# Decoder layer, one core: the end of a group's front moves into the network slots of the group before it

## What is computed

```python
x = layernorm(x + attn(x))                 # linear attention, 16 heads of 16, chunks of 64
x = layernorm(x + xattn(x, k, bias, ctx))  # a causal convolution over the channels
x = layernorm(x + ffn(x))                  # gate and up (256 -> 2048), gelu, product, down (2048 -> 256)

# xattn, for head size H = 16 groups of num_heads = 8 channels, all along L = 256
kv = v[:, :, :, None, :] * ctx[:, :, None, :, :]      # 8 x 8 products per group
y = causal_conv(kv, k) + kv * bias                    # the second term is the skip
out = einsum('bhijl,bhil->bhjl', y, ctx)
```

## Time and profile before

| | us |
|---|---|
| median of three runs | 573.89 (573.31 to 574.43) |
| the profiled execution | 574.71 |
| span of its instructions | 572.4 |
| PE busy in the span | 539.1 (94%) |
| DVE busy | 375.3 (66%) |
| ACT busy | 148.0 (26%) |
| POOL busy | 123.3 (22%) |

### The profile page before, as it was taken

The page is one execution under the profiler, slowest core; times in us unless marked ns, Lnnn a source line. Parts: engine busy times, 40 slices in busy tenths (PEclk is TensorE's granted clock), DMA queues, the critical chain, the costliest instruction groups (busy, mean ns, idle before and its releaser), DMA issues.

```text
span 572.4 us, 9307 instructions
## 1 busy us (share of the span) xinstructions
PE 539.1 (94%) x3385; PEld 439.7 (77%) x3385; DVE 375.3 (66%) x782; ACT 148.0 (26%) x259; POOL 123.3 (22%) x195
## 2 busy tenths in 40 slices
PE   5999979989989999999999999999999997699993
PEld 5766757766878888776888888866888885588883
DVE  3998888975876577875455668875454778533334
ACT  3422200252333112232232111332333110222230
POOL 2100078210002445120003444120003451200001
PEclk9999899999999999999999999999999999599998
DMA  5532342130110110023001110040001110100001
GB/s 173 156 80 79 89 118 66 38 111 2 48 45 29 46 50 26 0 78 108 1 1 38 56 40 16 0 147 0 0 0 46 55 46 2 37 1 0 1 0 37
DMA packets 25249, 26.69 MB, mean 47 GB/s; under 512 B 2816, under 2 KB 22784, under 8 KB 25216
## 3 DMA queue, kind: packets, MB, share of 16 engines
q1 hardware_dynamic: 14208, 15.73, 9.3%
q10 hardware_dynamic: 10576, 8.95, 5.1%
q0 software_dynamic: 432, 1.57, 0.8%
HBM read 24.15 MB, written 2.10 MB: 46 GB/s over the span
## 4 chain that ended last, share of the span: by engine, by line
PE 82%; DVE 9%; DMA 3%; issue 2%; POOL 1%; ACT 1%; ACTq 0%; POOLq 0%; DVEq 0%; SPq 0%
PE bank L911 17%; PE bank L913 15%; PE bank L912 15%; PE front_bank L1030 5%; PE front_bank L1033 4%; PE front_bank L1031 4%; PE front_bank L972 4%; PE front_bank L959 3%; PE bank L906 3%; PE front_bank L911 2%; PE front_bank L912 2%; PE front_bank L913 2%; PE front_bank L1004 2%; DVE st L719 1%; DMA wo_sb<-in_woT 1%
## 5 line engine op out<-in xcount | busy, mean ns | idle before, releaser
L911 PE MATMUL bank<-x2T_lo,ffn_hi 128*128 128x512 f32 x256 | 111.6, 436 | 4.1 <-DVE x2T_lo L838 4.1
L854 DVE TENSOR_TENSOR inter<-bank,inter 128x512 f32<-128x512 f32 x64 | 44.2, 690 | 95.6 <-PE bank L913 95.3
L913 PE MATMUL bank<-x2T_hi,ffn_hi 128*128 128x512 f32 x256 | 102.2, 399 | 0.0
L912 PE MATMUL bank<-x2T_hi,ffn_lo 128*128 128x512 f32 x256 | 101.9, 398 | 0.0
L436 POOL TENSOR_TENSOR qbd<-qT_sb,ctxT_sb 128x256 f32<-128x256 f32 x128 | 77.8, 631 | 76.8 <-PE front_bank L1033 63.3
L386 POOL TENSOR_TENSOR ve<-ve,minus_half 128x2 f32<-128x2 f32 x24 | 17.4, 743 | 301.0 <-DVE ve L726 229.8
L911 PE MATMUL bank<-ffn_lo,inter_hi 128*128 128x256 f32 x256 | 77.2, 302 | 0.8 <-DVE inter_lo L848 0.8
L588 ACT ACTIVATE inter_hi<-inter 128x512 fp32r<-128x512 f32 x64 | 40.4, 632 | 143.0 <-DVE inter L854 143.0
L582 ACT ACTIVATE inter<-bank 128x512 f32<-128x512 f32 x64 | 38.2, 598 | 134.5 <-PE bank L913 134.5
L913 PE MATMUL bank<-ffn_hi,inter_hi 128*128 128x256 f32 x256 | 72.0, 281 | 0.0
L912 PE MATMUL bank<-ffn_hi,inter_lo 128*128 128x256 f32 x256 | 71.9, 281 | 0.0
(11 more groups left out here) (115 smaller groups left out, 795.3 us busy)
## 6 DMA issues: line engine op xcount, KB each, us to landing
toep_sb<-in_toep ACTq DMA_DIRECT2D x64, 128.0 KB, 2.1
xT_sb<-in_xT SPq DMA_DIRECT2D x4, 512.0 KB, 6.3
ctxT_sb<-in_ctxT SPq DMA_DIRECT2D x4, 512.0 KB, 4.4
x_sb<-in_x SPq DMA_DIRECT2D x4, 512.0 KB, 5.3
ctx_sb<-in_ctx SPq DMA_DIRECT2D x4, 512.0 KB, 6.3
out<-ctxT_sb POOLq DMA_DIRECT2D x3, 512.0 KB, 3.4
raw_w<-in_gate_p SPq DMA_DIRECT2D x8, 128.0 KB
raw_s<-in_gate_s SPq DMA_DIRECT2D x8, 128.0 KB
```

Source lines behind the costliest of these rows:

```text
L854: nc.vector.tensor_tensor(inter[:, n % 2, :], up_ps[:, :], inter[:, n % 2, :], ALU.mult).then_inc(inter_ready, 1)
L911: nc.tensor.matmul(ps, w_hi, x_lo, start=start, stop=False, skip_group_check=True)
L912: nc.tensor.matmul(ps, w_lo, x_hi, start=False, stop=False, skip_group_check=True)
L913: return nc.tensor.matmul(ps, w_hi, x_hi, start=False, stop=stop, skip_group_check=True)
```

## The change

It moves steps, and changes no operation.

- The scores go three to a slot (slots 0 to 2), and all that follows stands one slot earlier: `conv` 0 in slot 9, four convolution steps in each of slots 10 to 12, three in slot 13.
- A new stage `join`, in six steps, takes slots 14 and 15: the last `conv_sum` and PE's skip products (step 0), the DVE skip multiplies and PE's transposes (1), the convolution's adds (2), the first skip add and its statistics (3), the second skip add (4), its statistics (5). They leave the turn.
- The stages of a slot are divided over the three parts as `i * n // 3`; a slot of four has its last two behind `down`.
- The skip products go to front banks 0 and 1, so they wait for the last `conv_sum` steps, and the next group's first projection waits for the skip multiplies (`sk_ready`).
- In the turn DVE does `split_x`, `total`, `normalise`, then its steps of the projections.

```diff
-        skip_ps = x2T_ps = psum[4:6]
+        x2T_ps = psum[4:6]
+        skip_ps = fb[0:2]
...
+        join = [("join", k) for k in range(6)]
+        for n in range(3):
+            slots[n] = scores[3 * n:3 * n + 3]
+        pause = ("pause", 0)
+        slots[3] = [("squares", 0), ("squares", 1), pause]
...
+        slots[9] = [pause, pause, conv[0]]
         for n in range(4):
-            slots[n] = scores[2 * n:2 * n + 2]
...
-        slots[4] = [scores[NU_S], ("squares", 0), ("squares", 1)]
...
-        slots[10] = [pause, pause, conv[0]]
-        for n in range(5):
-            slots[11 + n] = conv[3 * n + 1:3 * n + 4]
+            slots[10 + n] = conv[4 * n + 1:4 * n + 5]
+        slots[14], slots[15] = join[0:3], join[3:6]
...
-                        run(g, slots[s][i * each:(i + 1) * each])
+                        run(g, slots[s][i * n // 3:(i + 1) * n // 3])
...
+            def join(g, k):
+
+                if k == 0:
+                    conv_sum(g, CH - 1)
+                elif k == 1:
+                    for j in range(2):
+                        gated_skip(g, j)
+                elif k == 2:
+                    for j in range(2):
+                        add_conv(g, j)
+                elif k == 3:
+                    add_skip(g, 0)
+                    stats(g, 1, x_sb, 0)
+                elif k == 4:
+                    add_skip(g, 1)
+                else:
+                    count(dve, y_ready[1], 2, g, 2)
+                    stats(g, 1, x_sb, 1)
...
             def turn(done, prev, g, beside=nothing):
-                if prev is not None:
-                    conv_sum(prev, CH - 1)
                 if g is not None:
                     if not isinstance(g, int) or g:
                         split_x(g)
                 if done is not None:
                     total(done)
                 if prev is not None:
-                    x2_half(prev, 0)
-                    x2_rest(prev, 0)
-                if g is not None:
-                    proj(g, 1)
-                    beside(0)
...
                     normalise(prev, 1, x_sb, x2_sb)
+                if g is not None:
+                    for pair in range(3):
+                        proj(g, 2 * pair + 1)
+                        beside(pair)
...
                 if p == 0:
-                    count(pe, z_ready, 16, g, 0)
+                    count(pe, sk_ready, 2, g, 0)
...
-            def conv_out(g):
+            def join(g, k):
+
+                if k == 0:
+                    for j in range(2):
+                        count(pe, prod_ready, 2, g, j + 1)
+                        count(pe, z_ready, 16, g, CH - 1 + j)
...
+                elif k == 1:
+                    count(pe, conv_ready, 16, g, 16)
...
-                if prev is not None:
-                    conv_out(prev)
```

More of the change, by code:

```diff
@@ L259, in slot @@
             def slot(prev, g, s, times=(0, 0, 0)):
-                each = -(-len(slots[s]) // 3)
+                n = len(slots[s])
                 for i, part in enumerate((gate, up, down)):
@@ L769, in conv_sum @@
                     .then_inc(conv_ready, 1)
-            def x2_half(g, j):
-                both = x_sb[:, 2 * j:2 * j + 2].rearrange("p b f -> p (b f)")
-                ctx2 = ctx_sb[:, 2 * j:2 * j + 2].rearrange("p b f -> p (b f)")
+            def join(g, k):
[15 more added lines that the diff above has]
+                    stats(g, 1, x_sb, 1)
@@ L775, in x2_half, with pair_of, gated_skip, add_conv @@
+            def pair_of(tile, j):
+                return tile[:, 2 * j:2 * j + 2].rearrange("p b f -> p (b f)")
+            def gated_skip(g, j):
                 count(dve, skip_mm, 2, g, j + 1)
-                nc.vector.tensor_tensor(ctx2, skip_ps[j][:, :], ctx2, ALU.mult).then_inc(sk_ready, 1)
+                nc.vector.tensor_tensor(pair_of(ctx_sb, j), skip_ps[j][:, :], pair_of(ctx_sb, j), ALU.mult)\
+                    .then_inc(sk_ready, 1)
+            def add_conv(g, j):
                 count(dve, cT_mm, 2, g, j + 1)
-                nc.vector.tensor_tensor(both, fb[2 + j][:, :], both, ALU.add).then_inc(half_ready, 1)
@@ L780, in x2_rest, with add_skip @@
-            def x2_rest(g, j):
-                both = x_sb[:, 2 * j:2 * j + 2].rearrange("p b f -> p (b f)")
-                ctx2 = ctx_sb[:, 2 * j:2 * j + 2].rearrange("p b f -> p (b f)")
+                nc.vector.tensor_tensor(pair_of(x_sb, j), fb[2 + j][:, :], pair_of(x_sb, j), ALU.add)\
+                    .then_inc(half_ready, 1)
+            def add_skip(g, j):
                 count(dve, half_ready, 2, g, j + 1)
                 count(dve, sk_ready, 2, g, j + 1)
-                nc.vector.tensor_tensor(both, both, ctx2, ALU.add).then_inc(y_ready[1], 1)
-                count(dve, y_ready[1], 2, g, j + 1)
-                stats(g, 1, x_sb, j)
+                nc.vector.tensor_tensor(pair_of(x_sb, j), pair_of(x_sb, j), pair_of(ctx_sb, j), ALU.add)\
+                    .then_inc(y_ready[1], 1)
+                if j == 0:
+                    count(dve, y_ready[1], 2, g, 1)
@@ L881, in _ @@
             schedule(dve, turn, {"score": score, "rms": rms, "factor": factor, "outproj": outproj, "norm": norm,
-                                 "conv": conv}, nothing, inner, split, unpack, finish)
+                                 "conv": conv, "join": join}, nothing, inner, split, unpack, finish)
         @block.tensor
@@ L1122, in _ @@
             schedule(pe, turn, {"score": score, "sums": sums, "factor": factor, "outproj": outproj, "x1T": x1T,
-                                "conv": conv}, gate, up, down_before, nothing, lambda: down(G - 1, NT - 1, last_mm))
+                                "conv": conv, "join": join}, gate, up, down_before, nothing,
+                     lambda: down(G - 1, NT - 1, last_mm))
 def kernel(**inputs):
```

41 lines of the change are left out of this document (13 added, 28 removed).

## The result

The changed kernel took **589.0 us** as the median of 4 runs (587.71 to 590.5); the kernel before took 574.16 (573.31 to 576.87, 4 runs). The ratio is 1.0259, with a 95% interval of 1.0236 to 1.0282. It is slower, as forecast, but by 14.8 us and not by 10, and the median lies 1.0 us above the forecast's range (578.5 to 588.0). The profiled execution took 587.71, the fastest of the four; its span is 585.95 against 572.37, 13.6 more.

The account below looks back on a forecast made before the run. It took PE, busy 539.1 of 572.4 us, as the bound, so only idle time and low clock could be won. Terms -4.0 + 6.4 + 4.2 + 3.4 = +10.0 us gave a median of 583.9 us, range 578.5 to 588.0.

Parts of the forecast that it names:

- The two turns of the loop: In the loop's two turns PE waits 1.05 us before the last `down` and 0.65 for `xT_lo`: 3.4 us lost.
- Turn 2: The loop's turn in its first pass, last `down` to next network: 2.15 us shorter by the forecast's terms.
- turn 3: The same code in the loop's second pass: also 2.15 us shorter by the forecast's terms.
- What DVE no longer does in these turns was hidden, and stays worth nothing: In the loop's turns, DVE work taken out was hidden behind other work, so it gains 0.
- the packed convolution: Four convolution steps in a slot cost 0; moved stages keep their distances and so their cover.
- Turn 1: Group 0's join runs bare before the first projection: 3.8 us lost, plus 2.6 by a fallen clock, 6.4 in all.
- Last turn: From the last `down` to network 3: shorter by 3.5 us, and 0.4 less lost to the clock, 4.0 gained.
- the rival in which it holds: PE's clock stays up in the last turn, as its idle pieces are short: 580.7 us, chance 0.10.
- Scores: In slot 0, score 2 directly behind score 1 makes PE wait 1.4 us for the mask, three times: 4.2 lost.
- Networks: Networks 0 to 2 each grow 5.25 us: 2.8 skip products and transposes, 1.4 scores, 1.05 wait for `inter_lo`.
- A step costs PE 1.3 us wherever it stands: A convolution step takes PE 1.3 us in any place, so packing four to a slot adds 0.

Follow-up runs that it names:

- e1: The changed kernel with 55 more DVE instructions at its start, which only wait for a semaphore long there: 586.78 us, ratio 1.0209.
- e7: The changed kernel with the second half of the statistics moved from slot 15 behind `split_x`, and 56 cheap DVE instructions ahead of the loop: 582.05 us.
- e3: The kernel before the change with 30 more waiting DVE instructions at its start, 547 ahead of the loop: 577.48 us, ratio 1.006.
- e6: The changed kernel with two scores in slot 0, three each in slots 1 and 2, one in slot 3: 585.0 us, ratio 1.0188.
- e11: The kernel before with four convolution channels in slots 11 to 13, three in 14, none in 15: 578.43 us, ratio 1.0077.
- e8: The changed kernel with turn 1's join undone, scores and statistics moved, loop shifted, second skip add in the turn, finished group's statistics behind `x2T_lo`: 583.39 us.

## Why the prediction was right in part

**The two turns of the loop (forecast +3.4): the failed step.** Turn 2 was right to 0.4 us. For turn 3 the sentence "What DVE no longer does in these turns was hidden, and stays worth nothing", and the one behind the packed convolution, by which what is hidden keeps its cover, took the DVE program as free of cost in itself. The sum has no term for where the loop lies. DVE's branch back to the loop's head was worth 0 before and is worth 2.90 us after, and lies right ahead of the one DVE step that PE waits for; with 1.6 us of clock behind it, this makes 4.5 us. e1 took it away by placement alone (4.0 us of turn 3), e7 by placement together with the moved statistics (a turn 3 equal to turn 2), e3 put it into the kernel before by placement alone. That the place decides is shown; that it does so by a fetch of the loop's head is read from the packets' number and time, and was not tried by itself. No view of before showed the cost; what there was to see is 13 packets of instructions on q14, for several engines, and a branch in a loop of some 300 instructions.

The difference of the medians misses by 4.8 us, that of the stages by 3.5. The other 1.3 lies in no stage: of the changed kernel the fastest of four executions was profiled.

**Turn 1 (forecast +6.4, measured +5.0).** The mechanism was right: the first projection came at 109.09 (forecast 109.5), after a wait of 5.33, and 2.1 us came back before the network (forecast 2.0). Mis-sized was the clock behind it: low for 3.42 us, 1.7 lost, and not 2.6. The wait and the clock in the changed kernel, timeline and windows, against the earlier trace rows:

```profile
109.09 0.77 PE L925 MATMUL front_bank<-xT_lo,fold_hi 128*128 128x512 f32 x1 [5.33 <-DVE xT_lo L603]
```

```profile
103.50:108.86 5.36, 0.26 (x3) 0.02 (x1) 5.15 (x17) 0.00 (x0) 0.79 (x2) 1.00 0.20 71
108.86:112.28 3.42, 3.19 (x8) 2.54 (x9) 1.98 (x6) 0.25 (x1) 0.63 (x1) 0.50 0.12 11
```

I had taken the length of the last turn's low stretch for it; PE idled 5.33 us here and 6.36 there. That this length isn't fixed either shows in e6, whose turn 1 is the same: there the clock was low for 6.83 us, and network 0 starts 2.2 us later.

**Last turn (forecast -4.0).** From the last `down` to the network 7.37 us against 7.15. The clock fell, as chosen: the rival in which it holds is out. It fell behind the transposes, in the second idle piece. Timeline and windows of the changed kernel, against the earlier trace rows:

```profile
499.29 0.35 PE L925 MATMUL bank<-ffn_lo,inter_hi 128*128 128x256 f32 x1 [0.85 <-DVE inter_lo L862]
...
502.79 1.47 PE L1070 MATMUL bank<-ident,x_sb 128*128 128x128 f32 x8 [1.83 <-DVE x_sb L739]
...
506.66 0.77 PE L925 MATMUL bank<-x2T_lo,ffn_hi 128*128 128x512 f32 x1 [2.40 <-DVE x2T_lo L852]
```

```profile
504.81:506.66 1.85, 0.00 (x0) 0.03 (x1) 1.71 (x10) 0.46 (x1) 1.01 (x2) 0.50 0.00 0
506.66:511.64 4.98, 4.98 (x12) 3.92 (x13) 1.74 (x5) 0.60 (x1) 1.14 (x2) 0.50 0.31 109
```

The transposes still ran at full clock here (1.47 for eight, 1.95 before); the network's first 4.98 us did not, as before. Turn and network 3 together came out at -7.4, where -7.75 was forecast.

**Scores (forecast +4.2): right.** In the rows above the output product of score 1 starts 2.06 us behind score 1. In e6, where a gate matmul follows score 1, that one starts 0.64 behind it. The difference of 1.42 comes in three networks, 4.3; e6 gave 3.6 of it back in their spans.

**Networks (forecast 5.25 each): right by two errors that cancel.** In network 1 the skip products and transposes cost 2.11 in their new place and not 2.8, the wait in front of `down` about 0.8 and not 1.05, and the paired channels 0.7 to 0.8 and not 0. The sentence "A step costs PE 1.3 us wherever it stands" was wrong: a convolution step takes 1.11 with network parts on both sides and 1.28 as one of a pair. That the total of 5.25 came out is luck. e11 shows the last two of these; the first is read from the trace and was not tried by itself. Network 0 has 0.8 more than the others; 0.35 of it is a wait for `inter_lo` in slot 8, the rest is in pieces of 0.1 to 0.2 that I can't name.

## What to carry to other kernels

Read a turn of a loop in every pass, not once: equal code with unequal times between passes points at the branch, and a gap of "issue" behind it, with instruction packets at that very time, is the sign that the head of the loop had to be fetched. Whoever moves instructions on an engine with a loop moves that loop too, and the price, here 2.9 us and a clock that falls, comes or goes by a few dozen instructions. The step right behind the branch had better be one that nobody waits for; this is advice, and no run here tried it. And a bare stage takes the cover from others: fill the place in front of the last product of a chain, and before putting work in an engine's row look for the first instruction behind it that PE needs.

## What the runs showed of the hardware

- DVE's branch at the end of a loop of 296 to 298 instructions cost either nothing to 0.4 us or 2.5 to 2.9 us, in 13 kernels with nothing between the two. With a gap: 541, 547 and 549 instructions ahead of the loop, 18 or 19 packets on q14, two or three of them within 6 us around the branch: in all six kernels one starts about 1.0 us and one about 3.5 us behind it. Without: 517, 585, 587 and 596, 13 to 15 packets, and none from the branch to the end of the loop's second pass. Where the limits lie between 517 and 541, and between 549 and 585, was not tried. By the Trainium skill (Runtime: NRT & Kernel Launch, Instruction fetch mechanics) a page is a block of 256 instructions. Counted from the first instruction of DVE's program this doesn't give the pattern: 517 and 541 lie in the same block. Counted from another place it would. A loop of 296 to 298 instructions touches three blocks of 256 when its head lies in the last 40 or so of a block, and two otherwise; if a block began some 560 to 580 instructions into DVE's program, the heads at 541, 547 and 549 would be the only ones of the seven with three. This is an estimate from that size and the counts above, and no run tried it. The packets of q14 have 8 KB here (0.15 MB in 18), half of the 16 KiB that the section gives for a block, so the size is open too.
- Two channels of the convolution in a row (six matmuls of 256 columns each) take 2.56 us, and with parts of the network between 2.22, while PE reports no wait for either.
- A clock that falls behind an idle stretch of PE of 2.0 us (e8) costs as much again as the wait did: 2.0 and 1.6. Behind turn 1's wait of 5.3 us it was low for 3.41 us in the changed kernel and for 6.83 in e6, and in the last turn for 6.83 in the changed kernel and for 3.41 in e7, with the same idle times. This part of a sum can't be forecast better than to about 1.5 us.
